# Graph attention with a routed feed-forward network on one core: SyncE reads sixteen list positions with one register load, and drops the range assertions of the tile loop

## The reference

```python
x = x + gnn(layernorm(x), edges)          # 6250 nodes x 256, 8 heads of 32
x = x + ffn(layernorm(x)[None])[0]        # 16 experts, the best 2 of each node

# gnn, per edge src -> dst (206250 edges, sorted by dst)
scores = leaky_relu(s_src[src] + s_dst[dst], 0.2)
alpha = softmax of scores over the edges with one dst
out = segment_sum(hh[src] * alpha, dst) + x      # then LayerNorm, ELU

# ffn
topk_vals, topk_idx = top_k(x @ gate_w + gate_b, 2)
h = relu(x @ w1[e] + b1[e]);  y = x + sum over the 2 of softmax(topk_vals) * (h @ w2[e] + b2[e])
```

## Time and profile before

| what | value |
|---|---|
| three runs | 3191.4, 3192.68 and 3208.37 us, median 3192.68 |
| the profiled execution | 3186.81 us, of which the span of the trace is 3185.1 us |
| busy | POOL 1871.5 us (59%), PE 1771.6 (56%), DVE 1754.0 (55%), ACT 1115.8 (35%) |
| granted clock of TensorE, mean | 0.779 |
| edge stage, from its first gather to its last | 178.2 to 2619 us |
| transfers | 393.00 MB, mean 123 GB/s |

### The profile page before, as it was taken

How to read it: one execution, slowest core, us unless ns; L and a number is a source line. 1 busy time by engine, 2 the same in 40 slices (tenths; PEclk the granted TensorE clock), 3 DMA queues, 4 the chain that set the end, 5 groups by cost and what they waited for, 6 DMA issues and landing times. The chain is left out here.

```text
span 3185.1 us, 43688 instructions
## 1 busy us (share of the span) xinstructions
PE 1771.6 (56%) x9011; PEld 1444.0 (45%) x9012; DVE 1754.0 (55%) x4247; ACT 1115.8 (35%) x2079; POOL 1871.5 (59%) x1936
## 2 busy tenths in 40 slices
PE   6343545455454545445454545554454555899994
PEld 5232434343343434334343434343343434799993
DVE  6544546455554646555554645455564645665655
ACT  3323333333333333333333333342333332343433
POOL 2356666666666666666666666666666651555555
PEclk9667777776777777777777778777777767999997
DMA  5433344443434344343434444343443436433336
GB/s 189 114 114 111 108 127 122 111 125 109 127 110 128 107 125 126 110 127 107 125 110 124 122 113 124 110 125 107 129 123 110 125 97 207 127 106 99 107 104 247
DMA packets 185080, 393.00 MB, mean 123 GB/s; under 512 B 50833, under 2 KB 107626, under 8 KB 178772
## 3 DMA queue, kind: packets, MB, share of 16 engines
q0 software_dynamic: 90864, 262.34, 29.1%
q1 hardware_dynamic: 77524, 115.84, 11.8%
q10 hardware_dynamic: 16656, 14.43, 2.0%
HBM read 355.94 MB, written 36.52 MB: 123 GB/s over the span
## 5 line engine op out<-in xcount | busy, mean ns | idle before, releaser
L1267 POOL DMA_INDIRECT gat<-table,idx x1627 | 1546.8, 951 | 905.1 <-issue 471.7
L1366 PE MATMUL ps_sum<-msg,hot 128*128 128x264 f32 x3322 | 1097.6, 502 | 709.7 <-DVE msg L1413 449.1
L1366 PEld LDWEIGHTS ps_sum<-msg,hot 128*128 128x128 f32 x3322 | 829.7, 256 | 920.3 <-issue 726.3
L1413 DVE TENSOR_TENSOR msg<-gat,ps_weight 128x2304 f32<-128x2304 f32 x196 | 472.0, 2408 | 564.3 <-ACT ps_weight L1324 359.0
L1279 ACT ACTIVATE hotT<-dst_row,neg_id 128x4352 bf16<-128x4352 int16 x48 | 188.2, 3921 | 518.0 <-DMA dst_row<-dst_half 485.4
L1352 PE MATMUL ps_look<-dst_split,hotT 128*128 (+1 forms) x1661 | 80.8, 191 | 500.2 <-ACT hotT L1281 368.3
L1352 PEld LDWEIGHTS ps_look<-dst_split,hotT 128*128 128x128 bf16 x1661 | 67.2, 101 | 517.8 <-issue 489.3
L1566 DVE TENSOR_TENSOR num<-acc,ps_sum 128x264 f32<-128x264 f32 x49 | 21.0, 429 | 438.7 <-remote 241.9
L1410 DVE TENSOR_TENSOR hot<-ps_own,rel 128x1152 f32<-128x1152 f32 x196 | 250.2, 1277 | 0.0
L1324 ACT ACTIVATE ps_weight<-score 128x72 f32<-128x72 f32 x196 | 44.1, 225 | 508.7 <-DVE score L1404 494.8
L2130 PE MATMUL ps_ht<-xT,w_t 128*128 128x128 f32 x1712 | 214.5, 280 | 0.0
(11 more groups left out here) (412 smaller groups left out, 2135.4 us busy)
## 6 DMA issues: line engine op xcount, KB each, us to landing
dst_row<-dst_half SPq DMA_DIRECT2D x49, 1088.0 KB
gat<-table,idx POOLq DMA_INDIRECT x1661
b_t<-in_L_ffn_b_dram ACTq DMA_DIRECT2D x107, 128.0 KB
listing<-list_f SPq DMA_DIRECT2D x736, 0.5 KB
table<-rows SPq DMA_DIRECT2D x49, 128.0 KB, 1.7
y_rows<-y SPq DMA_DIRECT2D x48, 128.0 KB
x_all<-in_x_dram SPq DMA_DIRECT2D x6, 896.0 KB, 8.8
back<-chosen SPq DMA_DIRECT2D x3, 1792.0 KB, 17.6
```

The lines of the kernel that those rows point to most:

```text
L1267: pool.indirect_dma_start(gat[:, GSTART[g] + k, :], None, table, bass.IndirectOffsetOnAxis(ap=idx[g][:, k:k + 1], axis=0)).then_inc(landed ...
L1366: made = pe.matmul(ps_sum[:, 0:SUM], hot[:, m, k, :], msg[:, m, k, :], start=(g == 0 and k == 0), stop=(g == NG - 1 and k == n - 1))
L1413: dve.tensor_tensor(msg[:, m, 0:n, 0:D].rearrange("p j (h d) -> p j h d", d=HD), gat[:, j:j + n, 0:D].rearrange("p j (h d) -> p j h d", d=HD),
```

## The change

SP reads the 16 positions of `record` with one load into 16 registers, and neither they nor the two window starts of a tile get an assertion. The bounds are now only declared to the program that builds the kernel. The order of transfers and waits is the same.

```diff
             def window(t):
-                return sp.value_load(lo_i[0:1, bass.ds(t, 1)], min_val=0, max_val=E)
+                return sp.value_load(lo_i[0:1, bass.ds(t, 1)]).with_bounds(min_val=0, max_val=E)
...
         self.sent, self.listed = sem("sent"), sem("listed")
+        self.records = 0
...
         sp.wait_ge(self.list_ready, a + 1)
         sp.sem_inc(turn, 1)
         self.keep_gates(sp, a)
+        regs = [sp.alloc_register(name=f"list_at{self.records}_{e}") for e in range(EXPERTS)]
+        self.records += 1
+        sp.load(regs, self.base_i[0:1, 0:EXPERTS])
         for e in range(EXPERTS):
-            at = sp.value_load(self.base_i[0:1, e:e + 1], min_val=0, max_val=DROWS - P)
+            at = sp.snap(regs[e], donate=True).with_bounds(min_val=0, max_val=DROWS - P)
             sp.dma_start(self.lists[bass.ds(at, P)].unsqueeze(0), self.list_f[e:e + 1, :]).then_inc(self.listed, 16)
```

## The result

The changed kernel takes 3178.9 us (median of 6 runs, 3176.6 to 3188.5), the kernel before, run beside it, 3201.0 (6 runs, 3191.4 to 3208.4): a ratio of 0.9935, 95% interval 0.9913 to 0.9957. The profiled execution took 3177.5 us, 9.3 us less than the one shown ahead, about what was forecast.

A forecast was written before the change was run, and what follows sets the result against it. The prediction took POOL, with its waits on PE's signals, as the bound. It took 46 turns x 0.2 us = 9 us off the 3192.7 us median, giving 3184 us, with a range of 3090 to 3325 us.

The forecast's parts named there:

- POOL with its waits sets the pace, SP fits itself in: Per tile, 42.5 us of POOL's gathers plus 8.4 us of waits set the time; an earlier `hotT` gains little.
- 0.2 us a turn: Gain per tile with lists from an earlier `dst_row`, taken between nothing and 0.8 us; 46 turns give 9 us.
- Of the stages before and behind nothing changes: Outside the turns with lists, the stages before and behind were to add no gain or loss.
- What SP saves: On SP, instructions removed per tile were worth 12.4 us in a good stretch; less the new load, 5 to 12 us.
- The new load: SP's one load of sixteen positions was to cost some 2 to 3 us more, within bounds of 0.5 to 8.0.
- The list rows: SP's first to sixteenth list row were to fall from 22.7 us to 10 or less.
- The signs: `hotT`'s wait ends with PE or "remote"; POOL waits 2.6 us mid-g1, 3.5 to 5 mid-g3, none ahead of g3.
- The period: POOL's time per tile was to stay within 50 to 51 us, else the prediction is wrong.
- The first rival: Slower: POOL's pause mid-g1 goes, a dearer one mid-g2 comes; 3285 to 3360 us, chance 0.33.
- The point named for it: What decides the first rival: PE's g1 signal comes before POOL has issued half of g1.
- The second rival: Faster: POOL's g1 pause goes with nothing in its place, 2.3 us a turn; 3085 to 3170 us, chance 0.20.
- The third: SP is the pace, all five POOL waits shrink to nothing, 387 us less, 2806 us; chance 0.07.

The follow-up runs named there:

- the third occasion: The unchanged change timed once more, with the kernel before traced beside it: change 3182.7 us, kernel before 3189.0 us, ratio 0.9983.
- the twice loaded kernel: The kernel before with every list position loaded and asserted twice: 2991.7 us, ratio 1.0840; timed again 2992.2 us, ratio 1.0844.
- the parts alone: Against the kernel before: assertions alone removed, sixteen single loads kept, 3166.3 us, ratio 0.9950; one load alone, assertions kept, 3175.6 us, ratio 0.9977.
- the first occasion: The unchanged change timed again, 3183.3 us, ratio 1.0001 to the kernel before at 3186.1 us; its two parts were also timed separately.
- two stops: The changed kernel with POOL's mid-group stop for PE's sum kept in g1 and g3 alone: 2757.5 us, ratio 0.9990 to the kernel before.

## Why the prediction was right

**POOL with its waits sets the pace, SP fits itself in.** Right, on the chips with slow steps. In the changed kernel `hotT` starts 5.1 us sooner and a tile takes 51.06 us in the place of 50.92; in the two executions of the third occasion, 51.05 and 51.08. The kernel before shows the same inside one trace. Its 43 tiles, sorted by how late `hotT` starts and cut in three, have it 22.9, 26.6 and 27.9 us behind the first gather. The gap ahead of g3 grows with it (0.33, 1.10, 2.34), the one in the middle of g3 shrinks (3.81, 3.03, 1.83), and the tiles take 50.85, 50.92 and 50.99 us. The forecast gave 0.2 us a turn, 9 us in all; the three measured ratios come to 21 us less, nothing, and 5 us less, 9 us in the mean. The agreement is partly luck: in the profiled pair the 9 us didn't come from the turns at all, which had got longer by 0.14 us each, but from the first tiles, the last one and the stages behind, and these swing as much between executions of one kernel. "Of the stages before and behind nothing changes" holds for the program only.

**What SP saves.** In a good stretch sixteen rows take 6.20 us where 18.5 had been worked out from the earlier trace rows, 12.3 less; the first part of that term had 12.4 with the windows' pairs. The new load was put too high. It takes 1.17 us (0.70 by its median on the chip with slow steps, where some rows show next to nothing), 0.67 more than the single one, not 2 to 3. That is 0.045 us for each of the other fifteen registers, held against a single load of 0.50; the second load of the same position in the twice loaded kernel took 0.27, so what goes ahead of a load counts too. The Trainium skill (Runtime: NRT & Kernel Launch, Instruction fetch mechanics) gives about 200 ns per register, with the register loads in view that the runtime itself puts into a program. An estimate by it is 3.2 us. This load reads on-chip memory and took 1.17, and the measurement decides. What was missed is the other side. The list rows were to fall to 10 us or less, and fell to 15.7 in the mean: in a bad stretch register operations, moves and issues alike read 0.69 to 0.72 us each. Neither miss moved the time, since what SP saved went into its wait for `list_ready`.

**The signs.** ACT's wait ended with "remote", the gaps in the middle of g1 (2.6 us in the mean of the first trace) and of g3 (3.6) stayed, and the one ahead of g3 went, as written. The list rows didn't fall to 10 us. The period was to stay within 50 to 51 us and is 51.05 to 51.09 in the three traces of the change, a hair outside, with the kernel before at 50.92 and 51.08.

**The first rival** (g1's signal in time, a dearer pause in g2) was given 0.33 as an all-or-nothing case. It is real, but a matter of single tiles: none of 43 in the first trace, 6 and 7 in the others, with the price that the earlier trace rows gave (54.6 us for a tile there, 55.2 in the one shown, 52.8 to 55.6 in all thirteen). The point named for it, g1's signal there before POOL has issued half of g1, holds for the five in which that pause is all but gone; in the other eight it comes sooner than in a usual tile, but not that soon. In the kernel before none of 86 tiles did it. On the third occasion, held against the 51.08 us of the kernel before, the seven dear tiles cost 22 us and the 34 usual and skipping ones, at 50.4 in the mean, gave back 22. That is where the gain went in this execution. It isn't the whole reason why the parts alone beat the change on the first occasion: the first trace of the change has none of these tiles and a mean of 51.06 all the same. That stays open.

**The second rival** needs the pause of g1 to go with nothing in its place; no tile did that. **The third** (SP is the pace) was to give 2806 us, and 2759 is seen on two chips, but with the kernel before in its place: there POOL's waits are missing without any change. The nearest kernel with the change (two stops) stands at 0.999 of it. The loop through SP becomes the pace with 9 us more of work, and then at 47.4 us a tile.

## What to carry to other kernels

The longest idle time in the table, and the transfer that ends it, name what comes last and not what it is worth: look for two turns in the same trace in which it came early and late, and compare how long the pacing engine's turn was. A register load of many neighbouring positions is cheap against as many loads (1.17 us against sixteen of 0.50), but no run here shows it paying, since another loop was as long or longer; added loads cost time where they made the loop through SP the longest. Follow a saving from engine to engine, too, down to the signal that the pacing engine waits for: here PE was done 5 us sooner and its signal wasn't. And where waits decide, put the parts of a change and the change itself through more than one occasion before believing half a per cent.

## What the runs showed of the hardware

- **Two kinds of chip, or of occasion.** One program took 3186 to 3201 us on three occasions and 2759 us on two others. The busy times of POOL and PE over the steady tiles agree within 0.5% between the two (1390 and 1105 us in the kernel before on the one, 1385 and 1106 in the one with two stops on the other), and the mean granted clock of an execution is 0.78 in the one and 0.82 in the other. On the one kind instructions of SP that take 0.15 us rise to 0.72 and signals of PE lag by 2 to 4 us in the mean while gathers stream; on the other kind the same rows read 147/147/156 ns and 0.01 us. No chip on record was met twice, so whether the chip makes the difference or something else of the occasion isn't shown, and no run shows why.
- **Stops that help.** Where signals lag, the changed kernel without POOL's stops took 12% longer; where they don't lag, with half or a quarter of the stops left it took 0.999 of the kernel before.
- **Register loads.** One register 0.50 us behind the issue of a transfer and 0.27 behind an assertion, sixteen in one load 1.17; the pair of an assertion 0.147 + 0.018.
